# Another order of the steps in layer 1's attention pass, and a causal mask made by a select on POOL

## The reference, cut to what matters

```python
# layer 0 attention: 16 heads of 16
w = jnp.where(causal, jax.nn.relu(scores - ATTN_THRESHOLD), 0.0)
w = w / (jnp.sum(w, axis=-1, keepdims=True) + EPS)
out = w @ v
# layer 1 attention: 32 query heads, 8 key/value heads of 64, window of 64
q, k = rope(rms_norm(q, q_norm_w), rms_norm(k, k_norm_w))
scores = q @ k_rep.T * scale + sliding_mask
attn = softmax(scores) @ v_rep
y = attn @ w_out.T
```

## Time and profile before

| what | value |
|---|---|
| time, three runs | 682.22, 695.62 (median), 756.82 us |
| the profiled execution, its own time | 688.52 us |
| its span, first to last instruction | 686.7 us |
| mean clock granted to PE | 0.879 of full |
| POOL busy over the span | 278.5 us (41%) |
| ACT busy over the span | 345.1 us (50%) |
| layer 0 attention | about 10 to 126 us |
| layer 0 FFN | about 126 to 212 us |
| layer 1 attention, passes 3 to 21 | about 203 to 612 us |
| layer 1 FFN | about 612 us to the end |

### The profile page before, as it was taken

One profiled execution on the slowest core, in us unless ns is written; L12 is line 12 of the kernel. 1 busy time (PEld: TensorE's weight loads), 2 busy tenths in 40 slices (PEclk: granted clock), 3 DMA queues, 4 the chain that ended last, 5 costly groups with the idle time before them and its releaser, 6 DMA issues. The chain is left out here.

```text
span 686.7 us, 11172 instructions
## 1 busy us (share of the span) xinstructions
PE 556.4 (81%) x4040; PEld 473.3 (69%) x4040; DVE 477.6 (70%) x745; ACT 345.1 (50%) x956; POOL 278.5 (41%) x165
## 2 busy tenths in 40 slices
PE   4678989899997577797778779777778687899994
PEld 3534655788896566686767768676667676788884
DVE  4657778573638888887878878788788786444444
ACT  2455764345443284556546554753654646733221
POOL 3668665114315625632652463245263462240000
PEclk9778999999997688898898889889999768899998
DMA  8201000124100000000000000000101011100000
GB/s 294 64 29 32 1 30 2 45 95 114 48 1 0 1 1 16 16 2 15 16 17 2 15 17 1 17 17 1 31 17 31 16 47 34 64 12 1 1 31 31
DMA packets 8886, 21.11 MB, mean 31 GB/s; under 512 B 1280, under 2 KB 2944, under 8 KB 8704
## 3 DMA queue, kind: packets, MB, share of 16 engines
q1 hardware_dynamic: 8832, 20.40, 9.5%
HBM read 19.35 MB, written 1.05 MB: 30 GB/s over the span
## 5 line engine op out<-in xcount | busy, mean ns | idle before, releaser
L859 ACT ACTIVATE probs<-psum,minus_max 128x128 f32<-128x128 f32 x256 | 91.6, 384 | 136.2 <-DVE minus_max L1122 136.2
L1236 POOL TENSOR_TENSOR rope_sin_part<-qkv_rows,sin_weighted 128x640 f32<-128x640 f32 x32 | 63.2, 1996 | 182.9 <-DVE rope_cos_part L1084 115.7
L586 PE MATMUL psum<-identity,roped 128*128 128x128 f32 x128 | 31.0, 398 | 39.0 <-ACT probs L859 39.0
L908 DVE TENSOR_TENSOR out_t_low<-psum,out_t_high 128x512 fp32r<-128x512 f32 x36 | 24.8, 691 | 54.2 <-ACT out_t_high L870 53.9
L1245 POOL TENSOR_TENSOR rms_inverse<-rms_inverse,minus_half 128x20 f32<-128x20 f32 x16 | 57.4, 3587 | 1.3
L1116 DVE TENSOR_TENSOR probs<-probs,prob_inverse 128x512 f32<-128x512 f32 x64 | 56.3, 880 | 2.2
L859 ACT ACTIVATION_READ_ACCUMULATOR probs<-psum,minus_max 128x1 f32 x256 | 56.7, 221 | 0.0
L1209 POOL TENSOR_TENSOR weights_t<-weights_t,causal_block 128x512 f32<-128x512 f32 x32 | 45.3, 1441 | 26.4 <-DVE weights_t L952 20.2
L616 PE MATMUL psum<-identity,probs 128*128 128x128 f32 x256 | 48.2, 348 | 7.2 <-ACT probs L859 7.2
L586 PEld LDWEIGHTS psum<-identity,roped 128*128 128x128 f32 x128 | 21.7, 202 | 45.8 <-ACT probs L859 45.8
L386 PE MATMUL psum<-x_t_high,ug_high 128*128 128x512 f32 x128 | 51.5, 402 | 0.0
(11 more groups left out here) (156 smaller groups left out, 1723.7 us busy)
## 6 DMA issues: line engine op xcount, KB each, us to landing
raw_chunks<-in_ug SPq DMA_DIRECT2D x8, 512.0 KB, 3.8
raw_chunks<-in_wout SPq DMA_DIRECT2D x16, 256.0 KB, 2.7
raw_chunks<-in_qkv SPq DMA_DIRECT2D x8, 384.0 KB, 3.3
raw_chunks<-in_x SPq DMA_DIRECT2D x2, 512.0 KB, 5.4
raw_chunks<-in_w SPq DMA_DIRECT2D x2, 512.0 KB, 5.8
raw_chunks<-in_sel SPq DMA_DIRECT2D x2, 512.0 KB, 6.6
down_tree<-in_down SPq DMA_DIRECT2D x1, 1024.0 KB, 8.9
x_rows<-in_x_rows SPq DMA_DIRECT2D x2, 512.0 KB, 5.1
```

Of the source, the lines that this page charges most:

```text
L586: mm = nc.tensor.transpose(o[:, t * P:(t + 1) * P], qn[:, t, hp * P:(hp + 1) * P], ident[:])
L859: e = nc.scalar.activation(pr[:, c, q, :], o[:, q * P:(q + 1) * P], ACT.Exp, bias=negm[:, c, q:q + 1], accum_out=psum1[:, c, q:q + 1])
L1236: last = nc.gpsimd.tensor_tensor(ov[:, :, :, z, :], rv[:, :, :, 1 - z, :], sv[:, :, :, z, :], ALU.mult)
```

## The change: what it does

It gives the steps of a pass another order on PE, ACT and DVE, with the same steps and the same distances between groups (except that the projection of the first quarter, `proj1` 0, moves from the end of a pass to the beginning of the next). POOL's order stays. It writes out three waits: `turn1q` on PE waits for roped itself, since it now comes ahead of `turn1k`; `exps` on ACT waits for the transpose of the same quarter of the group before; `turn_p` on ACT waits for the pv1 of the group before. In layer 0 POOL's product with the constant tile becomes an affine_select of the same tile (keep where column minus row is at least 0, else 0), and the constant tile, its DMA and its wait go.

```diff
-TENSOR_PASS = [("turn1k", 4), ("turn1q", 4, 0), ("turn1q", 4, 1), ("turn_p", 5, 0), ("turn_p", 5, 1), ("out1", 6, 0),
-    ("proj1", 1, 1), ("scores1", 4, 0), ("pv1", 5, 0), ("turn_p", 5, 2), ("turn_p", 5, 3), ("proj1", 1, 2),
-    ("scores1", 4, 1), ("out1", 6, 1), ("pv1", 5, 1), ("proj1", 1, 3), ("proj1", 0, 0)]
-SCALAR_PASS = [("turn1k", 4), ("turn1q", 4, 0), ("turn1q", 4, 1), ("turn_p", 5, 0), ("turn_p", 5, 1), ("squares", 2),
-    ("proj1", 1, 1), ("exps", 4, 0), ("pv1", 5, 0), ("exps", 4, 1), ("turn_p", 5, 2), ("turn_p", 5, 3), ("wout", 5),
-    ("proj1", 1, 2), ("exps", 4, 2), ("pv1", 5, 1), ("exps", 4, 3), ("proj1", 1, 3), ("proj1", 0, 0)]
-VECTOR_PASS = [("turn1k", 4), ("turn1q", 4, 0), ("turn1q", 4, 1), ("probs", 5, 3), ("values1", 2), ("square_sums", 2),
-    ("maxima", 4, 0), ("maxima", 4, 1), ("pv1", 5, 0), ("rope_sums", 3), ("probs", 4, 0), ("normed", 3),
-    ("probs", 4, 1), ("maxima", 4, 2), ("maxima", 4, 3), ("pv1", 5, 1), ("cosines", 2), ("probs", 4, 2)]
+TENSOR_PASS = [("turn1q", 4, 1), ("out1", 6, 0), ("turn_p", 5, 0), ("turn1q", 4, 0), ("turn1k", 4), ("proj1", 1, 0),
+    ("proj1", 1, 1), ("turn_p", 5, 2), ("turn_p", 5, 1), ("scores1", 4, 0), ("pv1", 5, 0), ("scores1", 4, 1),
+    ("proj1", 1, 2), ("turn_p", 5, 3), ("proj1", 1, 3), ("out1", 6, 1), ("pv1", 5, 1)]
+SCALAR_PASS = [("turn1q", 4, 1), ("squares", 2), ("turn1k", 4), ("turn1q", 4, 0), ("turn_p", 5, 0), ("turn_p", 5, 1),
+    ("proj1", 1, 1), ("turn_p", 5, 2), ("proj1", 1, 0), ("exps", 4, 0), ("pv1", 5, 0), ("exps", 4, 1), ("proj1", 1,
+    2), ("wout", 5), ("turn_p", 5, 3), ("proj1", 1, 3), ("exps", 4, 2), ("exps", 4, 3), ("pv1", 5, 1)]
+VECTOR_PASS = [("turn1q", 4, 1), ("values1", 2), ("turn1k", 4), ("turn1q", 4, 0), ("rope_sums", 3), ("probs", 5, 3),
+    ("maxima", 4, 0), ("maxima", 4, 1), ("square_sums", 2), ("normed", 3), ("pv1", 5, 0), ("maxima", 4, 2), ("maxima",
+    4, 3), ("probs", 4, 0), ("probs", 4, 1), ("cosines", 2), ("probs", 4, 2), ("pv1", 5, 1)]
@@ PE
             def turn1q(k, hp):
 
+                pe.wait_ge(qn_done, k + 1)
                 o, done = claim(("turn1q", k, hp))
@@ SP
             for n in range(SLOTS):
                 load_chunk(n)
-            load_const(tri, "causal")
@@ ACT
             def exps(k, c):
                 o, done = take(act, ("scores1", k, c))
                 act.wait_ge(mx_done[c], k + 1)
+                if k:
+                    filled(act, ("turn1p", k - 1, c))
...
             def turn_p(k, c):
                 o, done = take(act, ("turn1p", k, c))
+                if k:
+                    filled(act, ("pv1", k - 1, c // 2))
@@ POOL
             def scores0(b, hg, part):
 
-                if b + hg + part == 0:
-                    pool.wait_ge(const_in["causal"], 16)
                 emptied(pool, *[("scores0", b, hg, part, h4) for h4 in range(HG)])
                 for kb in PART_BLOCKS[part]:
                     w = wt[:, hg % 2, :, W0_AT[kb]:W0_AT[kb] + P]
-                    nc.gpsimd.tensor_tensor(
-                        w, w, tri[:].rearrange("p (a q) -> p a q", a=1).to_broadcast([P, HG, P]),
-                        ALU.mult).then_inc(w_mask, 1)
+                    nc.gpsimd.affine_select(w, w, pattern=[[0, HG], [1, P]], compare_op=ALU.is_ge, fill=0.0, base=0,
+                                            channel_multiplier=-1).then_inc(w_mask, 1)
```

More of the change, by code:

```diff
@@ L198, in post_ln_two_layers @@
         had = keep("hadamard", [P], F32R)
-        tri = keep("causal_block", [P])
         eye2 = keep("eye_twice", [P], BF16)
@@ L312, in post_ln_two_layers @@
         const_in = {name: sem("in_" + name) for name in
-                    ("identity", "causal", "sign_ug", "sign_dp", "scale_ug", "scale_dp")}
+                    ("identity", "sign_ug", "sign_dp", "scale_ug", "scale_dp")}
         scales_set = sem("scales_set")
@@ L1293, in constants @@
         "identity": np.eye(P, dtype=f),
-        "causal": (p[None, :] >= p[:, None]).astype(f),
         "had": had.reshape(P, 1, P),
```

## The result

| | before | after |
|---|---|---|
| median of all runs | 692.15 us (682.22 to 756.82) | 573.87 us (568.68 to 576.29) |
| profiled execution, its span | 688.52, 686.7 | 574.04, 572.3 |
| PE's mean granted clock | 0.879 | 0.963 |

The ratio is 0.836 (95% interval 0.824 to 0.848); it compares the fast executions of either kernel, and 695.62 and 756.82 us of before were slow ones, so it is not the quotient of the two medians.

What follows compares the result with a forecast made beforehand. No engine's work bound a pass: DVE's waits and collisions with POOL, and PE's hole lowering its clock. Gain 88.5 in 14 periods plus 5 in the tail: 688.5-93.5 = 595, on the median's scale 601 us; range 585 to 650.

Steps and rivals of the forecast that it cites:

- the walk: Step-by-step count of PE, DVE and ACT through the new order of a layer 1 attention pass: period 17.0 us.
- one regular stop of PE at the step named: PE waits 0.75 us per pass ahead of pv1 for its ring bank, which ACT's copies must empty.
- a sign of being wrong: The prediction called itself wrong if PE waits for exps ahead of proj1 3 or turn1q, where 0.7 us were spare.
- 14 periods: Layer 1 attention's pass periods: 14 x 17.0 = 238, norm 6, transposes and half-filled first pass 4.5; 248.5 against 336.96 us.
- (a): Rival: PE's clock does not stay up in the passes; period 19.8, total 640 us; chance 0.14.
- (b): Rival: clock low for more than 0.42 of PE's pass work; old time at 0.42, 2% slower at 0.48; chance 0.02.
- (c): Rival: the wait moves, DVE waits for scores behind two proj1 and two turn_p; 18.8 per pass, 626 us; chance 0.13.
- (d): Rival: nothing gained, ring and reader meet as badly elsewhere; 6 us of new waits per pass, 685 to 695; chance 0.05.
- (e): Rival: slower by layer 0's select alone, 2% slower from 5.7 us each, 710 us; chance 0.03.
- tail: From 568.88 to 612.00, rest of pass 18 and passes 19 to 21: 5 of 43.12 us estimated gained.
- S: Zero of time in the counted pass: the start of the first half of scores1 on PE.
- no loss for pow: POOL's pow (3.5 us, 20 columns) lands on DVE's probs and cosines in a pass; no loss was counted for it.

Runs made afterwards that it cites:

- e4: Kernel before with POOL's product in sines replaced by a memset, leaving out the sine part of the rotation: 635.45 us, ratio 0.932.
- e7: Changed kernel with rope_sums on DVE moved right ahead of normed, so sines fall under normed again: 613.63 us, ratio 0.898.
- e3: Kernel before with 28 extra transposes on PE ahead of turn1k's own, filling PE's hole: 676.46 us, ratio 0.990.
- e5: Kernel before with only DVE's order new and the three waits written out: 608.46 us, ratio 0.892.
- e1: Kernel before with only POOL's mask as a select and without the constant tile: 682.26 against 684.43 us, ratio 0.9975.
- e2: Changed kernel with POOL's product and the constant tile put back, so only the new order and three waits: 572.93 us, ratio 0.8385.
- e8: Changed kernel without the two written waits on ACT, turn1q's kept only on the one now first: 569.58 us, ratio 0.8355.
- e9: Changed kernel with one ACT step moved, proj1 0 ahead of proj1 1 and turn_p 2: 571.34 us, ratio 0.8348.
- e10: Changed kernel with each mask select done four times in a row: 597.45 us, ratio 0.874.
- e11: Changed kernel with eight extra transposes on PE in each turn1k, 0.85 us per pass: 578.48 us, period 17.01.
- e12: Changed kernel with one extra maximum on DVE in each pass, 0.61 us: 574.79 us, period 16.42.
- e6: Kernel before with only PE's and ACT's orders new and the three waits: 704.48 us, ratio 1.031.

## Why the prediction was right in kind and too small

**Right.** The reading of what bounded a pass held: collisions (e4: 3.2 us, e7: 2.6 us), and a clock that mattered only as far as PE did (e3, e5). That the waits in DVE's own order are the rest is argued: DVE's order alone brings 5.0 us (e5), and no run parts them from the collisions in the new order. For the steady pass the walk was right in kind: sines under maxima and square_sums, the full clock, one regular stop of PE at the step named, nothing lost by the written waits, PE the bound with DVE close behind (0.3 us of waits, not 1.3). Outside it two things differ: PE did wait for exps ahead of turn1q in two early passes (0.87 and 0.84 us), which the prediction had named as a sign of being wrong, and the clock over the 14 periods is 0.97, 0.70 in the first of them. Rivals (a) and (b) fell: the clock is 1.00 over 128 us, with a stop of 0.36 us in every pass. The Trainium skill, "TensorE: Matmul & The Clock Gate", section "A second HAM failure mode: psum-queue depth-cycling", tells of a kernel whose clock swings by small idles between matmul groups as it cycles through PSUM banks. This stretch did not swing. (c) did not occur: DVE has no wait for scores in a steady pass; (d) fell, and so did (e), with 0.64 us for a select.

**Where the range failed.** Against the profiled 574.0 the sum of 595 was 21 us too high, and the step from there to 601 added 6 more. In the table the periods stand with their whole length, the other rows with their change against before, in us:

| step | forecast | measured | difference |
|---|---|---|---|
| 14 periods | 248.5 | 234.6 | -13.9 |
| start to layer 0's second ln_rstd (unchanged on to 175) | 0 | -2.5 | -2.5 |
| passes 1 to 3, and 3 to 4 | 0 | -4.9, -2.0 | -6.9 |
| tail | -5 | -2.6 | +2.4 |

*The period, 17.0 for 16.13, is the term that was mis-sized.* Two parts. PE's work was taken as 19.04-2.8 = 16.2; it is 15.77. The likely reason: the busy time before holds, at each stop, the recorded tail of the last matmul, which overlaps the next one when there is no stop. The distances between starts in the earlier trace rows, which the walk itself used, add up to 2 x 1.6 + 2 x 1.6 + 2 x 1.0 + 2 x 2.2 + 7 x 0.43 = 15.8 and should have been the sum. And the wait of PE was taken as 0.75 and is 0.36: ACT's first copy starts 0.10 us after S, not 0.3, and a copy of 384 columns takes less than one of 512 (0.37 against 0.48 from start to start). 0.43+0.39 = 0.82 of the 0.87; the 0.87 over 14 passes are 12 of the 13.9 us.

*Passes 1 to 4 were put at nothing, without a reason.* Every kernel with the old pass takes 37.26 us from the third ln_rstd to the first rope_sums (before, e1, e3, e4 within 0.02), every one with the new order on all three engines 32.33 (after, e2, e8, e9, e10, e11 within 0.01; e12 32.38). DVE's order alone takes 32.97 (e5), PE's and ACT's alone 36.23 (e6). e7, which differs from the changed kernel only in where rope_sums stands, takes 36.23 and 21.99 for the next period (17.61 after). So most of it is again that one step. DVE before:

```profile
210.89 1.49 DVE L1077 TENSOR_REDUCE square_sums<-squares 128x20 f32<-128x1280 f32 x1 [2.92 <-POOL rms_inverse L1245]
212.30 1.48 DVE L1084 TENSOR_TENSOR rope_cos_part<-rope_cos_part,rope_sin_part 128x1280 f32<-128x1280 f32 x1
...
214.42 2.54 DVE L1100 TENSOR_TENSOR roped<-rope_cos_part,rms_inverse 128x1024 f32<-128x1024 f32 x1
217.00 2.71 DVE L1071 TENSOR_TENSOR rope_cos_part<-qkv_rows,cos_weighted 128x1280 f32<-128x1280 f32 x1
```
and after:
```profile
204.88 1.49 DVE L1087 TENSOR_TENSOR rope_cos_part<-rope_cos_part,rope_sin_part 128x1280 f32<-128x1280 f32 x1
207.38 1.49 DVE L1080 TENSOR_REDUCE square_sums<-squares 128x20 f32<-128x1280 f32 x1 [1.00 <-POOL rms_inverse L1245]
208.78 2.10 DVE L1099 TENSOR_TENSOR roped<-rope_cos_part,rms_inverse 128x512 f32<-128x512 f32 x1
```
rope_sums no longer stands behind square_sums' wait for POOL's pow, so sines begin earlier and meet less of normed and cosines. The forecast had "no loss for pow" and did not ask who waits for it where the pipeline fills.

*The start, 2.5 us,* is within what the same code varies by (last section); the select's share is 1.7 us with an interval that reaches zero.

*The lower end.* The walk's own numbers gave a floor for the loop: the larger of PE's starts (15.8) and DVE's work (15.7) is 1.2 us below 17.0, 17 us in all, so 584. The range's low end of 585 has no more in it than that floor. It had no term for a gain ahead of pass 4 (6.9) nor for the start (2.5), and it rested on the three runs of before that were shown: in the later comparisons the median of before is 683.07 to 685.66 us, so the 1% added to come from the profiled execution to the median, 6 us, went the wrong way.

## What to carry to other kernels

When a loop's order is changed, price the new period as the larger of each engine's work at its shortest durations, from start to start and not from busy time, plus the waits that a walk through the order finds; and take the bare larger one as the lower end of the range. Look first at which two-input step of DVE lies under which of POOL's: here the place of one step was worth some 40 of the 114 us. An order belongs to all engines together: PE's and ACT's new ones without DVE's made the kernel slower.

## What the runs showed of the hardware that was not expected

A low clock costs only what PE's place on the path makes it cost: 0.45 us between two passes of e3, 1.5 in e5, 4.1 in the pass after the norm (e9). In the pass with the norm, where PE waits for DVE, it costs nothing: 22.36 us at 0.92 in the changed kernel's trace, 22.36 at 1.00 in e8's and e10's.

The same stop does not always bring the clock down. In e3 PE stops 2.48 us ahead of scores1 at 272.87 and at 295.80; the pass of the first has a clock of 1.00, that of the second 0.85. So the prediction's reading that a stop of 2.8 us lowers the clock and one of 1.3 does not is no rule, only what the kernel before showed.

The clock also differs between runs of the same instructions. In the head, windows of the kernel before and of e3, whose code is the same there:

```profile
9.00:28.00 19.00, 15.40 (x56) 13.06 (x56) 10.97 (x12) 4.85 (x8) 15.58 (x6) 0.84 0.48 175
28.00:52.00 24.00, 17.65 (x89) 10.13 (x88) 14.68 (x24) 13.72 (x23) 13.29 (x10) 0.77 0.14 44
```
```profile
9.00:28.00 19.00, 13.60 (x63) 10.64 (x63) 12.72 (x15) 8.49 (x14) 15.63 (x6) 0.95 0.46 163
28.00:52.00 24.00, 18.97 (x113) 10.97 (x117) 17.26 (x33) 12.62 (x22) 16.97 (x13) 0.82 0.15 45
```
The second norm's ln_rstd stands at 136.05 in the one and 128.88 in the other, 7 us apart, and over the traces taken here (e10 left out) anywhere from 127.75 to 136.05. Why the clock rises earlier in some runs was not tried. It means that marks in the head can't be compared between single traces, and that distances between marks in a steady stage can where the clock is the same: in the changed kernel and e2 all 14 periods agree within 0.03 us.

POOL's pow of 20 columns (L1245, 3.53 us at its shortest) does not slow DVE's two-input work, unlike sines, but is itself stretched by it: 3.92 us in the mean of the changed kernel, where probs and cosines (both with two inputs in SBUF) lie over it. One pass of it, DVE and POOL:

```profile
330.44 0.69 DVE L1119 TENSOR_TENSOR probs<-probs,prob_inverse 128x512 f32<-128x512 f32 x1
331.05 1.52 DVE L1074 TENSOR_TENSOR rope_cos_part<-qkv_rows,cos_weighted 128x1280 f32<-128x1280 f32 x1
```
```profile
330.47 4.06 POOL L1245 TENSOR_TENSOR rms_inverse<-rms_inverse,minus_half 128x20 f32<-128x20 f32 x1
```
